# Decoder layer on one core: x, keys, queries and values of the third and fourth pair made in front of the first up unit

## What is computed

```python
def reference(x, ctx_1024, ...):
    # attention, 16 heads of 16
    q = einsum('bsd,hde->bhse', x, wq) + bq   # k and v alike
    scores = softmax(einsum('bhse,bhte->bhst', q, k) * scale)
    att = einsum('bhst,bhte->bhse', scores, v)
    x = layernorm(x + att @ wo.T + bo)
    # recurrence over tokens: two scans A, Bm, decays exp(-w), exp(w)
    out = A + exp(u + k) * (v * Bm + max(t - 1, 0))
    x = layernorm(x + out)
    # experts: G, I = top_k(softmax(x @ Wg.T)), K = 128 of 128 tokens
    h1 = gelu(einsum('bekh,ehf->bekf', ex, W1) + b1)
    out = G * (einsum('bekf,efh->bekh', h1, W2) + b2)
    return layernorm(x + scatter_add(out))
```

## Time and profile before

| | |
|---|---|
| median of 3 runs | 917.84 us (917.34 to 917.88) |
| the profiled execution | 918.12 us, its span 916.4 us |
| PE busy | 876.4 us, 96% |
| PEld busy | 797.0 us, 87% |
| DVE busy | 586.0 us, 64% |
| ACT busy | 576.5 us, 63% |
| POOL busy | 80.4 us, 9% |
| granted PE clock, mean | 0.988 |

### The profile page before, as it was taken

How to read it: one execution, slowest core, us unless ns; L and a number is a source line. 1 busy time by engine, 2 the same in 40 slices (tenths; PEclk the granted TensorE clock), 3 DMA queues, 4 the chain that set the end, 5 groups by cost and what they waited for, 6 DMA issues and landing times.

```text
span 916.4 us, 17611 instructions
## 1 busy us (share of the span) xinstructions
PE 876.4 (96%) x6547; PEld 797.0 (87%) x6547; DVE 586.0 (64%) x1197; ACT 576.5 (63%) x969; POOL 80.4 (9%) x116
## 2 busy tenths in 40 slices
PE   6898888999999999999999999999999999999997
PEld 6788787889888999989988889889999889999997
DVE  6779798767656576665565674665676564333574
ACT  7568686766667455776557465765557665444684
POOL 4220012001010011000120010200120000000000
PEclk9999899999999999999999999999999999999999
DMA  8459999997738854686548954497537855665340
GB/s 250 154 191 338 352 311 312 285 301 244 240 109 244 242 174 132 178 231 212 174 127 230 235 169 146 134 231 239 181 118 181 250 183 169 190 187 177 103 139 12
DMA packets 195379, 185.00 MB, mean 202 GB/s; under 512 B 61896, under 2 KB 161504, under 8 KB 195296
## 3 DMA queue, kind: packets, MB, share of 16 engines
q1 hardware_dynamic: 195296, 183.88, 66.6%
HBM read 135.60 MB, written 35.65 MB: 187 GB/s over the span
## 4 chain that ended last, share of the span: by engine, by line
PE 76%; ACT 9%; DVE 5%; issue 2%; DMA 2%; SPq 1%; POOL 1%; POOLq 0%; ACTq 0%; DVEq 0%
PE down_ps L823 11%; PE down_ps L824 11%; PE down_ps L825 11%; PE up_ps L562 11%; PE up_ps L564 11%; PE up_ps L563 11%; DMA pt_lo<-p_lo 2%; ACT h_all L971 2%; PE bank L609 1%; ACT probs L912 1%; PE bank L584 1%; ACT L971 1%; PE bank L562 1%; PE bank L564 1%; PE bank L563 1%
## 5 line engine op out<-in xcount | busy, mean ns | idle before, releaser
L971 ACT ACTIVATE h_all<-up_ps,b_all 128x512 f32<-128x512 f32 (+1 forms) x296 | 182.3, 631 | 259.1 <-PE up_ps L564 250.0
L823 PE MATMUL down_ps<-w_hi,h_hi 128*128 128x256 f32 x1024 | 294.4, 288 | 4.4 <-DVE acc L1252 4.4
L1051 DVE TENSOR_TENSOR h_lo<-h_all,h_hi 128x512 fp32r<-128x512 f32 x256 | 176.3, 691 | 191.1 <-ACT h_hi L962 190.5
L824 PE MATMUL down_ps<-w_lo,h_hi 128*128 128x256 f32 x1024 | 289.8, 283 | 0.0
L825 PE MATMUL down_ps<-w_hi,h_lo 128*128 128x256 f32 x1024 | 289.7, 283 | 0.0
L562 PE MATMUL up_ps<-x2t_hi,w_hi 128*128 128x512 f32 (+1 forms) x588 | 220.1, 374 | 3.7 <-DVE x2t_lo L1051 1.9
L564 PE MATMUL up_ps<-x2t_hi,w_lo 128*128 128x512 f32 (+1 forms) x588 | 215.4, 366 | 0.0
L563 PE MATMUL up_ps<-x2t_lo,w_hi 128*128 128x512 f32 (+1 forms) x588 | 214.7, 365 | 0.0
L823 PEld LDWEIGHTS down_ps<-w_hi,h_hi 128*128 128x128 f32 x1024 | 195.1, 190 | 12.9 <-issue 3.0
L824 PEld LDWEIGHTS down_ps<-w_lo,h_hi 128*128 128x128 f32 x1024 | 195.9, 191 | 7.0
L825 PEld LDWEIGHTS down_ps<-w_hi,h_lo 128*128 128x128 f32 x1024 | 195.8, 191 | 0.0
(11 more groups left out here) (213 smaller groups left out, 953.9 us busy)
## 6 DMA issues: line engine op xcount, KB each, us to landing
w_hi<-w_parts SPq DMA_DIRECT2D x200, 256.0 KB, 3.3
w_lo<-w_parts SPq DMA_DIRECT2D x200, 256.0 KB, 3.5
w_raw<-in_w_dram SPq DMA_DIRECT2D x96, 256.0 KB, 4.1
w_parts<-w_hi SPq DMA_DIRECT2D x64, 256.0 KB, 4.0
w_parts<-w_lo SPq DMA_DIRECT2D x64, 256.0 KB, 4.2
x_in<-in_x_dram SPq DMA_DIRECT2D x8, 256.0 KB, 4.1
ctx_sb<-in_ctx_dram SPq DMA_DIRECT2D x8, 256.0 KB, 3.8
out_dram<-acc SPq DMA_DIRECT2D x8, 256.0 KB, 2.3
```

The lines of the kernel that those rows point to most:

```text
L823: nc.tensor.matmul(ps, hi, w2h[:, c, :], start=c == 0 and j == 0, stop=False, skip_group_check=True)
L824: nc.tensor.matmul(ps, hi, w2l[:, c, :], start=False, stop=False, skip_group_check=True)
L971: a = nc.scalar.activation(h_all[:, unit % HALL, k * wide:(k + 1) * wide], up_ps[unit % 2][:, k * wide:(k + 1) * wide], ACT.Gelu_apprx_tan ...
L1051: return nc.vector.tensor_tensor(dst, src, hi.bitcast(F32), ALU.subtract)
```

## The change

The steps `X`, `X_LOW`, `QK` and `V` of pairs 2 and 3 (`AHEAD = (2, 3)`) leave their items. In their place stand new steps in the hand-written order: `HEAD_X` (turn x), `HEAD_K_0` and `HEAD_K` (first and second half of the keys), `HEAD_Q`, `HEAD_V`. x of the two pairs is loaded by two DMAs of 256 KB early in the SP queue into `h_all`, and its split is kept in `h_hi` and `h_lo`, which are free until the first gelu. ACT copies each result (keys, queries, values, 128x512) out of PSUM: those of pair 2 into `p_hi` and `p_lo`, where they wait; those of pair 3 into `p_lo`, `acc` and `x2`, from where three DMAs of 256 KB write them to the DRAM tensor `heads` and three more read them back at pair 2's `ATT` (item 68). `K_COPY` and its kin stay where they were and read SBUF in place of PSUM. The idle products fall from 3 + 6 + 4 + 22 + 14 to 3 + 4 + 2. PE's order puts `R_TURN` of pair 0 between the first and the second scores of pair 1, which stood ahead of it. The Gelu table load moves behind four of the new ACT copies.

```diff
+        def laid_by(p, i):
+            if place_ahead(p) == 0:
+                return landing(i)
+            return (rows_of(p_lo, 1), acc[:, 1]..., x2_all[:, 1]...)[i]
+        def ahead_bank(p, s):
+            return {HEAD_X: up_ps[1], HEAD_K_0: (bank[3], up_ps[1])[place_ahead(p)], HEAD_K: (bank[3], up_ps[1])[place_ahead(p)], HEAD_Q: (bank[1], bank[3])[place_ahead(p)],
+                    HEAD_V: (bank[2], up_ps[1])[place_ahead(p)]}[s]
...
+            for p in AHEAD:
+                load_x_ahead(p)
...
             load_ctx(1)
+            for p in AHEAD[1:]:
+                store_heads(p)
...
-                        if s == QK and p > 1 and p + 1 < NPAIR:
+                        if s == K_COPY and p > 1 and p + 1 < NPAIR:
                             load_x(p + 1)
+                        if s == ATT and p + 1 in AHEAD[1:]:
+                            load_heads(p + 1)
...
+            def go_ahead(p, s):
+                a = place_ahead(p)
+                ps = ahead_bank(p, s)
+                if s == HEAD_X:
+                    pe.wait_ge(x_ahead_loaded[a], 16)
+                    if a == 0:
+                        pe.wait_ge(pt_ready, 2 * 3)
+                    else:
+                        pe.wait_ge(xt_ready, p)
+                    turn(by_chunk(ps), x_ahead(p)).then_inc(xt_ps, 1)
+                    return
...
+                if s == HEAD_Q:
+                    if a == 0:
+                        pe.wait_ge(ctx_t_ready, 1)
+                    else:
+                        pe.wait_ge(head_laid, 1)
...
+                if s == HEAD_V:
+                    if a == 0:
+                        pe.wait_ge(att_t_ready, 1)
+                    else:
+                        pe.wait_ge(head_laid, 3 + 1)
...
                 if s == SCORES[0]:
+                    if second(p):
+                        pe.wait_ge(head_laid, 3 + 2)
...
                 if (p, s) == (0, W_3):
-                    idle_products(bank[3], 6)
+                    idle_products(bank[3], 4)
                 if (p, s) == (0, CTX):
-                    idle_products(bank[3], 4)
-                if (p, s) == (1, V):
-                    pe.wait_ge(ctx_t_ready, 1)
-                    idle_products(bank[1], 22)
-                if (p, s) == (0, BACK):
-                    idle_products(bank[1], 14)
+                    idle_products(bank[3], 2)
...
+                if s in HEAD:
+                    act.wait_ge(head_ps, 3 * place_ahead(p) + HEAD.index(s) + 1)
+                    nc.scalar.activation(laid_by(p, HEAD.index(s)), ahead_bank(p, s), ACT.Copy).then_inc(head_laid, 1)
...
-            + [(1, X), (0, W_3), (0, ATT), (0, CTX), (0, WO), (1, QK), (0, Y1), (1, V), (0, BACK), (1, S_0), (1, S_1), (0, R_TURN)])
+            + [(1, X), (0, W_3), (2, HEAD_X), (0, ATT), (0, CTX), (3, HEAD_X), (0, WO), (1, QK), (2, HEAD_K_0), (0, Y1), (1, V),
+               (2, HEAD_K), (2, HEAD_Q), (2, HEAD_V), (3, HEAD_K_0), (3, HEAD_K), (0, BACK), (3, HEAD_Q), (3, HEAD_V), (1, S_0),
+               (0, R_TURN), (1, S_1)])
...
-             + [(1, X), (0, ATT), (0, CTX), (1, K_COPY), (0, XEXP), (1, Q_COPY), (1, DIAG_0), (1, DIAG_1), (0, R_TURN)])
+             + [(1, X), (2, HEAD_X), (0, ATT), (0, CTX), (3, HEAD_X), (1, K_COPY), (0, XEXP), (1, Q_COPY), (1, DIAG_0), (1, DIAG_1),
+                (2, HEAD_K), (2, HEAD_Q), (2, HEAD_V), (3, HEAD_K), (3, HEAD_Q), (3, HEAD_V), (0, R_TURN)])
...
+AHEAD = (2, 3)
```

More of the change, by code:

```diff
@@ L118, in places @@
             return {}
[L119 to L121 removed]
+        at = EARLY[p - 1] if p <= len(EARLY) else {s: FIRST_ITEM[JOIN[p]] + at for s, at in STEADY.items()}
+        return {s: item for s, item in at.items() if p not in AHEAD or s not in (X, X_LOW, QK, V)}
     AT = [places(p) for p in range(NPAIR)]
@@ L286, in decoder_layer @@
         ctx_loaded = sem("ctx_loaded")
+        x_ahead_loaded = [sem(f"x_ahead_loaded{i}") for i in range(len(AHEAD))]
+        head_ps = sem("head_ps")
+        head_laid = sem("head_laid")
+        heads_stored = sem("heads_stored")
+        heads_loaded = sem("heads_loaded")
         xt_ps = sem("xt_ps")
@@ L385, in by_dma, with ahead, place_ahead, x_ahead @@
             return p >= 2
+        def ahead(p):
+            return p in AHEAD
+        def place_ahead(p):
+            return AHEAD.index(p)
+        def x_ahead(p):
+            return h_all[:, place_ahead(p), :].rearrange("p (j d) -> p j d", j=PAIR)
+        def xt(p):
+            if ahead(p):
+                return by_chunk(h_hi[:, place_ahead(p), :]), by_chunk(h_lo[:, place_ahead(p), :])
+            return xt_hi[:], xt_lo[:]
+        def rows_of(t, half):
+            return t[:, half].rearrange("p i h t -> p (i h t)").bitcast(F32)
+        def landing(i):
+            return rows_of((p_hi, p_hi, p_lo)[i], i % 2)
+        def laid_by(p, i):
+            if place_ahead(p) == 0:
+                return landing(i)
+            return (rows_of(p_lo, 1), acc[:, 1].rearrange("p j d -> p (j d)"), x2_all[:, 1].rearrange("p j d -> p (j d)"))[i]
+        def ahead_bank(p, s):
+            return {HEAD_X: up_ps[1], HEAD_K_0: (bank[3], up_ps[1])[place_ahead(p)], HEAD_K: (bank[3], up_ps[1])[place_ahead(p)], HEAD_Q: (bank[1], bank[3])[place_ahead(p)],
+                    HEAD_V: (bank[2], up_ps[1])[place_ahead(p)]}[s]
         def turns(p):
@@ L569, in project @@
                     mm = product(ps, proj_hi[:, which, kc, cols], proj_lo[:, which, kc, cols],
-                                 xt_hi[:, kc, :], xt_lo[:, kc, :], kc == 0, kc == C - 1)
+                                 x_hi[:, kc, :], x_lo[:, kc, :], kc == 0, kc == C - 1)
                 return mm
@@ L724, in route @@
                     pe.wait_ge(x2_ready, b + 1)
+                    if first(b):
+                        pe.wait_ge(head_laid, 2)
                     for c in range(C):
@@ L782, in up @@
                 weights(n, 0, u * G // units(n))
+                if unit == 1:
+                    pe.wait_ge(head_laid, 3 * len(AHEAD))
                 if unit >= 2:
@@ L1099, in attend @@
                 x_ps, _, _, v_bank = head_banks(p)
-                if s == X_LOW:
+                if ahead(p):
+                    x_ps, v_bank = ahead_bank(p, HEAD_X), landing(2)
+                if s in (X_LOW, HEAD_X):
                     dve.wait_ge(xt_hi_ready, p + 1)
-                    low(xt_lo[:], by_chunk(x_ps), xt_hi[:]).then_inc(xt_ready, 1)
+                    low(xt(p)[1], by_chunk(x_ps), xt(p)[0]).then_inc(xt_ready, 1)
                 for c in range(C):
@@ L1112, in attend @@
                         dve.wait_ge(bv_loaded, 16)
-                    dve.wait_ge(v_ps, p + 1)
+                    if not ahead(p):
+                        dve.wait_ge(v_ps, p + 1 - (len(AHEAD) if p > 1 else 0))
+                    elif place_ahead(p) == 0:
+                        dve.wait_ge(head_laid, 3)
+                    else:
+                        dve.wait_ge(heads_loaded, 16 * 3 * place_ahead(p))
                     for j in range(PAIR):
@@ L1409 @@
  ATT, CTX, WO, NORM1, Y1, XEXP, REC_0, REC_1, REC_2, REC_3, BACK, NORM2,
- R_TURN, R_LOGITS, R_MAX, R_GATE, R_GATE_T, R_BIAS, K_LOW_1, Q_LOW_1) = range(53)
+ R_TURN, R_LOGITS, R_MAX, R_GATE, R_GATE_T, R_BIAS, K_LOW_1, Q_LOW_1, HEAD_X, HEAD_K_0, HEAD_K, HEAD_Q, HEAD_V) = range(58)
 DIAGONAL = (DIAG_0, DIAG_1)
```

67 lines of the change are left out of this document (54 added, 13 removed).

## The result

The changed kernel takes 911.69 us (median of 5 runs, 910.21 to 913.17) against 917.84 us before in the same session; the ratio is 0.9929, 95% interval 0.9912 to 0.9946. The profiled execution took 912.31 us with a span of 910.5: 5.9 us of span are gone. The prediction was 911.4, in a range of 908.9 to 914.8.

A forecast was written before the change was run, and what follows sets the result against it. The prediction took PE to bound the kernel from about 190 us on, ACT and DVE mostly ahead of that; -0.4 - 0.5 - 5.6 = -6.5 us against the profiled 918.1 gave 911.6, stated as 911.4, range 908.9 to 914.8.

The forecast's parts named there:

- a sign by which the prediction called itself wrong: Behind 255 us: the prediction is wrong if the lead there is lost again by waits on weights or DMA.
- Up to the first up unit, -0.4: Hand-written part: `R_TURN` starts at 51.95 in place of 52.38 us, no longer behind all scores; -0.4 us.
- Pair 2, -0.5: 113 to 132 us: PE's 4.6 us count nothing, ACT loses `xt_hi` ahead of a table load; -0.5 us, bounds 0 and -1.3.
- POOL's chain would end at 143.9: After `v_all`: POOL's chain was to end 1 us earlier than before, at 143.9 us.
- Pair 3, -5.6: 236 to 252 us, PE-bound: 4.6 us of PE work and a 1.07 us wait behind `xt_lo` leave; -5.6 us.
- No wait behind 250 us: By 255 us PE is 6.5 us ahead and keeps that; no PE wait on a weight shows after 250 us.
- (a): Rival: clock falls ahead of pair 0's `WO` for 6 us from about 34 us, 3 us late; 914.4 us, 12%.
- (b): Rival: thinned stretch 120.9 to 138.5 us runs cold; 6 us costs 0 to 1, lasting until 155 gives 920.8; 3%.
- (c): Rival: pair 2's PE work counts because ACT and DVE are fed sooner; half of 4.6 us gives 909.1; 12%.
- like time from fewer clock falls: First 170 us: the clock falling less often elsewhere, worth up to 2.5 us, gives a time like 909.1.
- (d): Rival: pair 3's gain held up by ACT, a weight piece or reads back of heads; -3.3 us, 914.8, 10%.
- (e): Rival: a load of x for `HEAD_X` lands late and holds pair 0's attention; 911.6 plus the lateness, 1%.

The follow-up runs named there:

- after: The changed kernel in its first measurement and trace, against the kernel ahead of the change: 911.69 us, ratio 0.9929.
- experiment 3: Two runs on the order of `R_TURN`: the new order alone in the unchanged kernel, 918.48 us; the old order in the changed kernel, 911.52 us.
- left_p2: Unchanged kernel with pair 2's projections reduced to one matmul for each result, so its output is wrong: 918.87 us.
- before: The kernel without the change: 917.84 us in the session of the result, medians of 916.79 to 919.53 us by session.
- left_p3: Unchanged kernel with pair 3's projections reduced to one matmul for each result, so its output is wrong: 915.89 us, ratio 0.9967.
- after_again: The changed kernel measured and traced a second time, nothing altered: 912.18 us, ratio 0.9919.
- old_order: Changed kernel with pair 0's `R_TURN` back behind pair 1's second scores: 911.52 us.
- no_dram: Changed kernel without the three stores and three loads of pair 3's heads; pair 3 reads pair 2's heads instead: 911.68 us.
- no_idle: Changed kernel without the last 4 + 2 idle products around pair 0's `att` and `ctx`: 910.27 us.
- act_late: Changed kernel with six more 128x512 copies on ACT ahead of the copy of pair 3's keys: 912.86 us.
- order_only: Unchanged kernel with only pair 0's `R_TURN` moved between pair 1's first and second scores: 918.48 us.
- fill_att: Changed kernel with 16 idle products in PE's wait for pair 1's `att`: 911.24 us, ratio 0.9917.
- w2_later: Changed kernel with `W_2` at -29 in place of -30 in STEADY, one down unit later: 908.17 us, ratio 0.9888.
- both_waits: Changed kernel with 16 idle products ahead of pair 1's `att` and `W_2` one down unit later: 910.02 us, ratio 0.9902.
- three_waits: both_waits plus 16 idle products ahead of pair 1's `mix` and 7 ahead of its first shared up unit: 906.57 us, ratio 0.9855.

## Why the prediction was right, point by point

**The total.** Forecast -6.5 us against the profiled run, measured -5.8 (912.31 against 918.12) and, between medians, -6.15. Two of the three steps fit within 0.02 us, and the third was 0.45 too small. That the total fits is partly luck, since three terms that were not in the sum came in as well. In after the lag of -5.9 at the end is +0.75 (late start) - 0.39 - 0.38 (clock at 104 us) - 0.50 - 6.05 + 0.66 (given back behind 256 us); the last of these was a sign by which the prediction called itself wrong, and it came true in part.

**Up to the first up unit, -0.4.** Measured -0.39 in both runs. Right in size and place; the reason, the order of `R_TURN`, is one of two that each suffice (experiment 3). `R_TURN` was forecast at 52.0 and the first up unit at 53.2; they came at 52.73 and 53.96, all of it the late start of 0.75.

**Pair 2, -0.5.** Measured -0.50 in both runs between 112 and 120 us, where ACT's `xt_hi` stood, and nothing from there to 232 us. PE's work there costs nothing, as left_p2 showed with 3.5 us of it. I said that POOL's chain would end at 143.9, the 144.82 of before less the first two steps (0.9). The scores behind it start at 144.32: both steps came, but the late start of 0.75 us, of which the clock at 104 us gave back 0.38, stands against them.

**Pair 3, -5.6: the term that was mis-sized.** Measured -6.05 to -6.06 from 232 to 256 us. The trace of before closes it if one reads starts rather than brackets. The starts, beside the earlier trace rows:

```profile
240.85 0.28 PE L825 MATMUL down_ps<-w_hi,h_lo 128*128 128x256 f32 x1
...
245.13 0.39 PE L562 MATMUL up_ps<-x2t_hi,w_hi 128*128 128x512 f32 x1
...
251.63 0.28 PE L823 MATMUL down_ps<-w_hi,h_hi 128*128 128x256 f32 x1
```

`X` costs 0.36, and the up unit behind it 0.08 more for starting anew; the last down matmul starts at 240.85, so the next would have at 240.97, and queries and keys start at 242.20: 1.23, not 1.07, since a bracket counts from the modelled end of a matmul that overlaps the next; 242.20 to 245.13 is 2.93, not 2.8; the values 250.09 to 251.63, less 0.11 that the next matmul pays now, 1.43. Sum 6.03. I also rounded 5.67 down. Of this left_p3 shows 3.6 us by experiment; the rest, the wait above all, is read from the two traces.

**No wait behind 250 us: the term that was missing.** The prediction took the lead of 6.5 at 255 us as kept. It was 6.5 to 6.6 there, but the `pt_lo` waits took 0.9 at 292 us and gave and took up to 0.9 later. They were in the earlier trace rows and I gave them no range: each depends on a DMA that takes 3.1 to 5.8 us from issue to landing in after (median 3.9). Which of the five is long is hardly chance: in all six traces of after and of the kernels that equal it behind 60 us or nearly so (after_again, old_order, no_dram, no_idle, act_late) the long ones are at 290 to 293 us (1.2 to 1.5 us) and at 608 to 610 (1.0 to 1.3), and in before and order_only one at 510 us (1.2 to 1.3). So the give-back recurs with the changed kernel. But in fill_att, which has the same code behind 128 us and stood 0.9 us later at 256 us, the same two were 0.2 and 0.4 us; what makes them long is open. w2_later shows that the five were a term of 3 us in after; before has five of them too, 2.5 us, on which no run was made.

**The rivals.** (a) did not happen, and no_idle shows it was far off. (b) did, in its harmless form: PE stood at half clock from 126.6 to 133.4 us, in a stretch with slack, at no cost (lag -0.52 at 120 us, -0.49 at 232). (c) is out by left_p2, though the "like time from fewer clock falls" is real: in six of the twelve runs the stretch at 104 us lasted 3.4 us in place of 6.8 and the lag was 0.9 better. Two of the six, w2_later and left_p3, are up to there the same program as after and before, which had 6.8, so it is chance. (d) is out for DRAM by no_dram; the give-back was of its kind, though from another DMA. (e): no wait on x shows.

## What to carry to other kernels

Price a step by what ends the next wait behind its place: the same 31 matmuls cost 0.0 us where ACT and DVE set the pace and 3.6 us where PE does, and there all of pair 3's steps, wait included, cost 6 us. Moving such work to a place where the engine has nothing to do can be worth as much as removing it. Read costs from start to start, and when several edits remove one delay, check each alone before adding them up. A lead won early must pass every wait behind it: list the waits that remain, small as they are, because a one-item shift of the consumer (w2_later, 3.5 us in the trace, 2.8 between medians) can be worth half of a large rewrite. When you fill one long wait of PE, look at where the clock falls next: here filling one wait won nothing in the end, and filling three did.

## What the runs showed of the hardware

PE's stretches of low clock lasted 3.4, 6.8, 10.2 or 13.6 us in these traces (the longest from 16.9 to 30.5 us, in no_dram). Whether the one at 104 us was short or long followed no edit, and was worth 0.9 us. By 32 us the kernels differed by 2 us (lag -0.91 to +0.97 against before), and most of that is scatter between executions: the six traces whose code is the same up to 100 us (after, after_again, w2_later, fill_att, both_waits, three_waits) lie between -0.42 and +0.97.

Sixteen idle products in a 4 us wait kept the clock full there (2.4 us of gain). A wait need not be that long for a fall to follow: in all fourteen traces a wait of 2.00 us for `acc` ends at 154.3 to 157.3 us, and the clock falls for 3.4 us within 1.3 us of its end. Yet the wait of 2.02 us at 184 to 187 us was followed by a fall in fill_att and three_waits and by none in the other twelve.
